# Latent attention of a decoder kernel: turns as a loop of eight, and turns written out with exponentials per head

## The chip, the cores and the metric

The kernel runs on one core of a Trainium2 chip. The metric is the device time of one execution in microseconds; three runs of the kernel before have a median of 2204.88 us (2204.24 to 2206.10). The program is one launch that holds a whole stack of four layers; the change is in one of its eight stages, with a small part moved into the set-up at the start.

## The reference

x is 4 sequences of 512 tokens with 128 features, the context 4 times 77 keys with 128 features. Each of the four layers adds a cross attention and a feed-forward of experts to x. The stage that changes is the cross attention of layer 1:

```python
xn = layernorm(context, ln_x_g, ln_x_b); ln = layernorm(x, ln_l_g, ln_l_b)
q = (ln @ Wq)                                       # 16 heads of 64
kv = concat([xn @ Wkv, ln @ Wkv], axis=1)           # 77 context keys and 512 tokens as keys
qn = rmsnorm(q, qn_g) * 64 ** -0.5; kn = rmsnorm(k, kn_g)
sim = where(mask, einsum('bhid,bhjd->bhij', qn, kn), -max)
out = softmax(sim) @ v ; x = x + out.reshape(b, 512, 1024) @ Wout + bout
```

All of it is float32; products that need it are taken from a high and a low part (float32r) of each operand.

## The kernel before

The 16 heads are taken in 8 pairs, and each pair with each of the 4 sequences is a turn: 32 turns, b = turn % 4. A turn has five chunks of keys, four of 128 tokens and one of the 77 context keys (k = 4). TensorE computes transposed scores, keys down the partitions, for both heads of the pair side by side: head 0 uses partitions 0 to 63 of the operands, head 1 the others. `scores` (L1350) does three matmul pairs for a chunk and a fourth that subtracts the row maximum (`lead`), into banks 0 and 1 or 2 and 3 by turns; `exps` on ScalarE (L1517) makes probabilities of them in one instruction of 128x1024; `add` on GpSimd (L1244) sums these over the chunks in four additions; `product` (L1373) multiplies them by the values into bank 6.

The maximum comes a turn ahead: `bound` (L1330) multiplies the high parts of queries and keys of turn + 1 into banks 4 and 5, and `read_bound` on VectorE (L1616) reduces them before the next `bound` may write there; after chunk 4 a small addition of two 128x8 tiles (an ALU maximum, L1625) writes `top_wide`. Beside this TensorE has "side products" that all pass through bank 7, each waiting until the one before it has been read: keys KL and queries Q of turn + 2, the sums of squares NKL and NQL (for the norms, by a matrix of ones), values V4, the sum SUM and the output Y of turn - 1, the transpose MT of `top_wide`, and in three turns of four one of KC, NKC, VC for the context keys and values of the next pair. VectorE copies keys and queries out of the bank, scales them by the inverse norm and splits the queries (`part_queries`, L1655: `q_hat`, `q_high`, `q_low`); GpSimd splits the keys (`part_keys`, L1232, and `part_context`); ScalarE does squares, logarithms and exponentials of the norms.

Each engine's order is written out by hand as the body of a loop of eight turns (two pairs), run four times, with semaphore targets computed in registers; the names of this stage's tiles in the profile are `sb_L_...`. The last passes also do KL, Q and bounds for turns that do not exist, whose results nobody uses. A prologue ahead of the loop norms the context and the tokens, clears tiles on GpSimd and does the first side products. `move` copies each pair's split weights inside SBUF from a store to a place of fixed address.

Of the kernel before, what the change touches and what calls it, by code (L numbers as in the profile page):

```python
# [23 lines left out]
P = 128  # L24
# [87 lines left out]
def constants(c):  # L112

    nc, d = c.nc, c.dram
    loaded, built = c.sem("loaded"), c.sem("built")
    counts = c.ctx.enter_context(nc.sbuf_tensor("counts", [P, 12], mybir.dt.int32))
    with nc.Block() as block:
        @block.sync
        def _(sp):
            sp.dma_start(c.resid[:], d["x"]).then_inc(loaded, 16)  # L120
            sp.dma_start(c.vecs[:], d["vecs"]).then_inc(loaded, 16)
            sp.dma_start(c.rows[:], d["rows"]).then_inc(loaded, 16)
            sp.dma_start(c.ctxT[:], d["ctxT"]).then_inc(loaded, 16)
            sp.wait_ge(loaded, 64)

        @block.gpsimd
        def _(pool):
# [15 lines left out]
            step(pool.memset(c.pairsum[64:128, 64:128], 1.0))  # L143


class Norm:
# [27 lines left out]
    def vector(self, dve):  # L174
# [32 lines left out]
        for b in range(BATCH if self.split else 0):  # L207
            self.wait(dve, b)
            at = slice(b * SEQ, (b + 1) * SEQ)
            step(dve.tensor_copy(self.high[:, at], c.normT[:, at]))  # L210
            dve.tensor_tensor(self.low[:, at], c.normT[:, at], self.high[:, at], ALU.subtract).then_inc(self.parted, 1)
# [10 lines left out]
    def scalar(self, act):  # L222
        act.wait_ge(self.var_ready, 1)
        act.activation(self.std[:], self.work[:, 1, :], ACT.Sqrt).then_inc(self.std_ready, 1)
        if self.inner_eps is not None:
            act.wait_ge(self.var_ready, 2)
            act.activation(self.std2[:], self.work[:, 2, :], ACT.Sqrt).then_inc(self.std_ready, 1)
        scale = self.rstd if self.inner_eps is None else self.scale
# [866 lines left out]
def latent_attention(c):  # L1095
# [7 lines left out]
    LOOP = 2 * BATCH  # L1103

    KL, Q, NKL, NQL, V4, SUM, Y, MT, KC, NKC, VC = range(11)
    BY_DVE = (KL, Q, Y, MT, KC)
    PROLOGUE = [(KC, 0), (VC, 2), (NKC, 1), (KL, 7), (Q, 6), (NKL, 3), (NQL, 0), (V4, 1), (KL, 2), (Q, 7), (NKL, 6), (NQL, 3), (MT, 7)]
    EXTRA = (KC, NKC, VC, None)
    LOOPED = [kind for j in range(LOOP) for kind in (KL, NKL, Q, SUM, NQL, V4, EXTRA[j % BATCH], Y, MT) if kind is not None]
    STARTS = [sum(9 - (i % BATCH == BATCH - 1) for i in range(j)) for j in range(LOOP + 1)]  # L1110
    AHEAD_EXPS, AHEAD_ADDS, AHEAD_PV = 6, 4, 5

    with ExitStack() as ctx:
        norm = Norm(c, ctx, "L1", inner_eps=1e-5, gain=c.vec("L1_lg"), shift=c.vec("L1_lb"), split=True)
        w_all = c.sb(ctx, "L1_w_all", [P, PAIRS + 1, 2, P])
# [974 lines left out]
```

## Time and profile before

| what | us |
|---|---|
| median of three runs | 2204.88 |
| profiled execution | 2210.48 |
| its span, first to last instruction | 2208.6 |
| TensorE / VectorE / ScalarE / GpSimd busy in it | 1911.2 / 1267.7 / 853.2 / 678.6 |
| mean granted TensorE clock | 0.941 of 2.4 GHz |
| latent attention, first instruction to last addition | 409.3 to 1186.9 |

A time in the profile is a position from the span's start. The row of an instruction has its start and duration, and in brackets how long its engine was idle ahead of it and what ended that. A matmul's end is modelled. In a stage where four engines work in a fixed order, a busy share does not say who is waited for; the rows of one turn, engine by engine, do.

### The profile page before, as it was taken

What the parts mean: (1) busy time and instruction counts of PE and PEld (TensorE: products, weight loads), DVE (VectorE), ACT (ScalarE), POOL (GpSimd) and SP (SyncE); (2) the same over time, 40 slices, a digit from 0 to 9 for tenths busy, and PEclk for the clock granted to TensorE, in tenths of its full rate; (3) what the DMA queues carried; (4) which work ended last, traced back from release to release, by engine and by line L of the source; (5) the groups of instructions that cost most, each with busy time, mean ns of one, the idle gap of its engine ahead of it and who ended that gap; (6) DMA issues with size and microseconds to landing.
All of it is one profiled execution on the core that took longest, in us unless ns stands there. A gap on an engine that the chain in (4) does not pass through costs nothing. (4 is left out here: it accounts for less than half of the span.)

```text
span 2208.6 us, 35547 instructions
## 1 busy us (share of the span) xinstructions
PE 1911.2 (87%) x12346; PEld 1335.2 (60%) x12346; DVE 1267.7 (57%) x2588; ACT 853.2 (39%) x1278; POOL 678.6 (31%) x458
## 2 busy tenths in 40 slices
PE   4978999479989989998996999959869999969798
PEld 2547999334444444444443788835546789947697
DVE  4755111556656565655665544459779975547533
ACT  2553434245545544554554222225510030045443
POOL 3321110335555564655563011033321222012110
PEclk9997999779999999999998899979979999979899
DMA  1000000100000000000000000000010000000000
GB/s 35 1 15 7 28 19 10 35 0 8 8 2 8 8 2 8 1 8 9 1 3 20 11 19 19 10 17 1 1 30 19 24 29 15 0 20 0 15 20 29
DMA packets 19844, 28.54 MB, mean 13 GB/s; under 512 B 3356, under 2 KB 13497, under 8 KB 19462
## 3 DMA queue, kind: packets, MB, share of 16 engines
q1 hardware_dynamic: 19718, 26.86, 3.9%
q8 instruction: 79, 1.29, 0.2%
q14 instruction: 47, 0.39, 0.1%
HBM read 23.71 MB, written 1.05 MB: 11 GB/s over the span
## 5 line engine op out<-in xcount | busy, mean ns | idle before, releaser
L1253 POOL TENSOR_TENSOR sb_L_total<-sb_L_total,sb_L_probT 128x1024 f32<-128x1024 f32 (+1 forms) x96 | 227.5, 2370 | 127.1 <-ACT sb_L_probT L1527 64.7
L1619 DVE TENSOR_REDUCE sb_L_top_tok<-banks 128x2 f32<-128x1024 f32 x132 | 161.8, 1226 | 81.2 <-PE banks L1339 81.1
L1525 ACT ACTIVATE sb_L_probT<-banks 128x1024 f32<-128x1024 f32 x128 | 130.0, 1015 | 120.1 <-PE banks L1370 112.3
L350 POOL TENSOR_TENSOR sb_L_prob<-sb_L_prob,sb_L_rsum 128x616 f32<-128x616 f32 (+1 forms) x96 | 98.1, 1045 | 227.0 <-DVE sb_L_rsum L566 227.0
L1380 PE MATMUL banks<-sb_L_probT,sb_L_v 128*64 128x512 f32 x520 | 138.2, 611 | 0.0
L1919 DVE SCALAR_TENSOR_TENSOR sb_L2f_hid<-banks,sb_L2f_weight,sb_L2f_hid 128x512 f32<-128x512 f32 x192 | 134.7, 744 | 3.2 <-PE banks L88 1.9
L1018 ACT ACTIVATE sb_L0f_hidden<-banks,sb_L0f_b 128x512 f32<-128x512 f32 x128 | 87.8, 689 | 112.8 <-PE banks L88 111.5
L1046 DVE SCALAR_TENSOR_TENSOR sb_resid<-banks,sb_L0f_weight,sb_resid 128x128 f32<-128x128 f32 x128 | 36.1, 344 | 164.5 <-PE banks L966 163.9
L1249 POOL TENSOR_TENSOR sb_L_total<-sb_L_probT 128x1024 f32<-128x1024 f32 x32 | 76.2, 2380 | 163.7 <-ACT sb_L_probT L1525 163.7
L966 PEld LDWEIGHTS banks<-sb_L0f_w,sb_L0f_hidden 128*128 128x128 f32 x1024 | 119.7, 192 | 2.8
L492 ACT ACTIVATE sb_L_probT<-banks 77x512 f32<-77x512 f32 x160 | 89.9, 590 | 80.7 <-PE banks L402 80.7
L1015 ACT ACTIVATE sb_L1f_gate<-banks 112x512 f32<-112x512 f32 x96 | 57.4, 598 | 162.5 <-PE banks L88 162.5
L966 PE MATMUL banks<-sb_L0f_w,sb_L0f_hidden 128*128 128x128 f32 x1024 | 119.8, 275 | 0.0
L1991 DVE SCALAR_TENSOR_TENSOR sb_resid<-banks,sb_L2f_weight,sb_resid 128x128 f32<-128x128 f32 x192 | 67.4, 351 | 69.2 <-PE banks L88 50.5
L388 PE MATMUL banks<-sb_L_kdiag,sb_L_qT 128*128 (+2 forms) x192 | 85.2, 586 | 17.2 <-DVE sb_L_prob L557 9.0
L966 PEld LDWEIGHTS banks<-sb_L1f_w,sb_L1f_hidden 112*128 112x128 f32 x768 | 92.1, 195 | 7.5 <-DVEq L1076 4.4
L966 PE MATMUL banks<-sb_L1f_w,sb_L1f_hidden 112*128 112x128 f32 x768 | 92.5, 278 | 3.9 <-DVEq L1076 3.9
L1060 DVE TENSOR_TENSOR sb_L1f_hidden<-sb_L1f_gate,banks 112x512 f32<-112x512 f32 x96 | 65.8, 687 | 49.5 <-PE banks L88 47.1
L402 PE MATMUL banks<-sb_ident,sb_L_prob 128*77 128x128 f32 x640 | 93.1, 280 | 0.0
L86 PE MATMUL banks<-sb_L2f_w_high,sb_L2f_norm_low 128*128 128x512 f32 x192 | 81.6, 425 | 9.8 <-DVE sb_L2f_hid L1919 9.6
L86 PE MATMUL banks<-sb_L2f_w_high,sb_L2f_hidT_low 128*128 128x384 f32 x256 | 86.3, 337 | 1.7 <-DVEq L1982 1.7
L88 PE MATMUL banks<-sb_L2f_w_high,sb_L2f_hidT_high 128*128 128x384 f32 x256 | 86.1, 336 | 0.0
(460 smaller groups left out, 4589.6 us busy)
## 6 DMA issues: line engine op xcount, KB each, us to landing
sb_L2f_w<-L2f_w SPq DMA_DIRECT2D x12, 256.0 KB, 2.6
sb_L2f_w<-L2f_w SPq DMA_DIRECT2D x4, 768.0 KB, 4.3
sb_L1f_w<-L1f_gu SPq DMA_DIRECT2D x8, 336.0 KB, 3.0
sb_L0f_w<-L0f_w SPq DMA_DIRECT2D x8, 259.0 KB, 2.7
sb_L0f_w<-L0f_w SPq DMA_DIRECT2D x8, 256.0 KB, 2.9
sb_L1f_w<-L1f_dn SPq DMA_DIRECT2D x8, 168.0 KB, 2.9
sb_L3f_w<-L3f_w SPq DMA_DIRECT2D x9, 129.0 KB, 2.1
sb_L3f_w<-L3f_w SPq DMA_DIRECT2D x9, 128.0 KB, 2.2
```

Of the source, the lines that this page charges most:

```text
L86: pe.matmul(out, sl, mh, start=start, stop=False)
L88: return pe.matmul(out, sh, mh, start=False, stop=stop)
L350: pool.tensor_tensor(grid, grid, bcast(rsum[:, i % PROBS, half], [None, KEYS]), ALU.mult).then_inc(normed, 1)
L402: last = pe.transpose(ps[0:KEYS, TURN + g % 2, a * P:(a + 1) * P], prob[:, i, h * KEYS:(h + 1) * KEYS], c.ident[:])
L492: act.activation(probT[:, g * GROUP:(g + 1) * GROUP, :].rearrange("k h t -> k (h t)"), ps[0:KEYS, TURN + g % 2, :], ACT.Copy).then_inc(tur ...
L966: last = pe.matmul(ps[:, YBANK + b % 2, t * P:(t + 1) * P], hid[:, b % 2, f, t * P:(t + 1) * P], w2[:, u, f, :], start=(f == 0), stop=(f = ...
L1018: act.activation(hid[:, b % 2, f, :], ps[0:R, slot, :], func, bias=bias).then_inc(hid_ready, 1)
L1253: pool.tensor_tensor(sums[rows], sums[rows], probT[rows, k], ALU.add).then_inc(added, 1)
L1380: last = pe.matmul(O[HEAD[h]], v[:, w, k, HEAD[h]], probT[:, k, h, :], start=(k == 0), stop=False)
L1525: act.activation(probT[:, k], ps[:, slot:slot + 2, :], ACT.Exp).then_inc(exped, 1)
L1619: ins = dve.tensor_reduce(top_tok[:, :, k:k + 1].rearrange("p h k -> p (h k)"), ps[:, 4:6, :], AX.X, ALU.max)
L1919: dve.scalar_tensor_tensor(out=hid[:, n, :], in0=ps[:, n % BANKS, :], scalar=flat[:, bass.ds(n * L + e, 1)], in1=hid[:, n, :], op0=ALU.mul ...
```

## The change

- The loop of eight turns becomes 32 turns written out, with constant semaphore targets; work for turns that do not exist is left out. All pairs' weights stay in SBUF, loaded once.
- `exps` makes one instruction per head, and `scores` and `product` wait and signal per head.
- TensorE's `bound` of chunk 4 stands behind V4, product 0 and the side product of the context, and VectorE's `read_bound` of chunk 4 behind `scale_context` and `part_queries`. The copy of the context keys goes from VectorE to ScalarE.
- The context's norm, transposes and clears (`LatentContext`) run in the set-up block at the kernel's start; x is loaded behind the context there.
- In the prologue the bounds of turn 0 use two pairs of banks, and GpSimd splits the first pair's weights first and the others behind the keys of turn 1; VectorE splits the last two sequences' tokens behind the queries of turn 1.

```diff
@@ -109,19 +109,21 @@
     return ap.broadcast_to(shape)
 
 
-def constants(c):
+def constants(c, early):
 
     nc, d = c.nc, c.dram
-    loaded, built = c.sem("loaded"), c.sem("built")
+    loaded, built, vecs_in, ident_ready = c.sem("loaded"), c.sem("built"), c.sem("vecs_in"), c.sem("ident_ready")
     counts = c.ctx.enter_context(nc.sbuf_tensor("counts", [P, 12], mybir.dt.int32))
+    made = LatentContext(c, early)
     with nc.Block() as block:
         @block.sync
         def _(sp):
+            sp.dma_start(c.vecs[:], d["vecs"]).then_inc(vecs_in, 16)
+            made.sync(sp)
             sp.dma_start(c.resid[:], d["x"]).then_inc(loaded, 16)
-            sp.dma_start(c.vecs[:], d["vecs"]).then_inc(loaded, 16)
             sp.dma_start(c.rows[:], d["rows"]).then_inc(loaded, 16)
             sp.dma_start(c.ctxT[:], d["ctxT"]).then_inc(loaded, 16)
-            sp.wait_ge(loaded, 64)
+            sp.wait_ge(loaded, 48)
 
...
+            pool.engine_nop().then_inc(ident_ready, 1)
+            made.gpsimd(pool)
+
+        @block.tensor
+        def _(pe):
+            pe.wait_ge(ident_ready, 1)
+            made.tensor(pe)
+
+        @block.scalar
+        def _(act):
+            made.scalar(act, vecs_in)
+
+        @block.vector
+        def _(dve):
+            dve.wait_ge(ident_ready, 1)
+            made.vector(dve, vecs_in)
+
+    return made
 
...
-            step(dve.tensor_copy(self.high[:, at], c.normT[:, at]))
-            dve.tensor_tensor(self.low[:, at], c.normT[:, at], self.high[:, at], ALU.subtract).then_inc(self.parted, 1)
+        self.step = step
+        for b in range(parts if self.split else 0):
+            self.part(dve, b)
+
...
+class LatentContext:
...
+    def tensor(self, pe):
+        pe.wait_ge(self.staged, 1)
+        for b in range(BATCH):
+            last = pe.transpose(self.c.ps[:, 0, b * KEYS:(b + 1) * KEYS], self.stage[:, b, :], self.c.ident[0:KEYS, 0:KEYS])
+        last.then_inc(self.turned, 1)
...
+        w_all, wv, wo = c.sb(ctx, "L1_w_all", [P, PAIRS, 2, P]), c.sb(ctx, "L1_wv", [P, PAIRS, P]), c.sb(ctx, "L1_wo", [P, PAIRS, P])
+        w_high, w_low = (c.sb(ctx, f"L1_w_{n}", [P, PAIRS, 2, P], F32R) for n in ("high", "low"))
...
-                def scores(turn, j, b, u, w, k, lead_read=None):
-                    n = turn * CHUNKS + k
-                    pe.wait_ge(exped, n - 1 + AHEAD_EXPS)
-                    slot = (j * CHUNKS + k) % 2 * 2
+                def scores(turn, k):
+                    n, p, b = turn * CHUNKS + k, turn // BATCH, turn % BATCH
+                    slot, rows = n % 2 * 2, rows_of(k)
                     if k < TPB:
-                        rows = P
                         high, low = (x[:, b, k * P:(k + 1) * P] for x in (k_high, k_low))
                     else:
-                        rows = KEYS
-                        high, low = (x[:, u, b, 0:KEYS] for x in (kc_high, kc_low))
-                    at = [ps[0:rows, slot + h, :] for h in range(2)]
+                        high, low = (x[:, p % 2, b, 0:KEYS] for x in (kc_high, kc_low))
+                    to = [ps[0:rows, slot + h, :] for h in range(2)]
                     for h in range(2):
-                        pe.matmul(at[h], low[HEAD[h]], q_high[HEAD[h], b, :], start=True, stop=False)
+                        if n >= 2:
+                            pe.wait_ge(exped, (n - 2) * 2 + h + 1)
+                        pe.matmul(to[h], low[HEAD[h]], q_high[HEAD[h], b, :], start=True, stop=False)
                     for h in range(2):
-                        pe.matmul(at[h], high[HEAD[h]], q_low[HEAD[h], b, :], start=False, stop=False)
+                        pe.matmul(to[h], high[HEAD[h]], q_low[HEAD[h], b, :], start=False, stop=False)
                     for h in range(2):
-                        pe.matmul(at[h], high[HEAD[h]], q_high[HEAD[h], b, :], start=False, stop=False)
+                        pe.matmul(to[h], high[HEAD[h]], q_high[HEAD[h], b, :], start=False, stop=False)
                     if k == 0:
-                        pe.wait_ge(dve_read, lead_read)
+                        wait_read(pe, MT, turn)
                     for h in range(2):
-                        last = pe.matmul(at[h], ones[HEAD[h], 0:rows], lead[HEAD[h], w, :], start=False, stop=True)
-                    last.then_inc(scored, 1)
-
-                def product(turn, b, u, w, k):
-                    n = turn * CHUNKS + k
-                    pe.wait_ge(exped, n + 1 + AHEAD_EXPS)
-                    if k == 0:
-                        pe.wait_ge(mixed_ready, turn + 1)
+                        pe.matmul(to[h], made.ones[HEAD[h], 0:rows], lead[HEAD[h], turn % 2, :], start=False, stop=True).then_inc(scored, 1)
+
+                def product(turn, k):
+                    p, b = turn // BATCH, turn % BATCH
+                    if k == 0 and turn > 0:
+                        pe.wait_ge(mixed_ready, turn)
                     for h in range(2):
+                        pe.wait_ge(exped, (turn * CHUNKS + k) * 2 + h + 1)
                         if k < TPB:
-                            last = pe.matmul(O[HEAD[h]], v[:, w, k, HEAD[h]], probT[:, k, h, :], start=(k == 0), stop=False)
+                            last = pe.matmul(O[HEAD[h]], v[:, turn % 2, k, HEAD[h]], probT[:, k, h, :], start=(k == 0), stop=False)
                         else:
-                            last = pe.matmul(O[HEAD[h]], vc[:, u, b, HEAD[h]], probT[0:KEYS, k, h, :], start=False, stop=True)
+                            last = pe.matmul(O[HEAD[h]], vc[:, p % 2, b, HEAD[h]], probT[0:KEYS, k, h, :], start=False, stop=True)
                     last.then_inc(pv_done, 1)
...
+                    scores(turn, 3)
+                    if more:
+                        bound(turn + 1, 3)
+                        use_side(V4, turn + 1)
+                    product(turn, 0)
+                    if p + 1 < PAIRS and b < BATCH - 1:
+                        use_side((KC, NKC, VC)[b], p + 1)
+                    if more:
+                        bound(turn + 1, 4)
+                    scores(turn, 4)
+                    if turn > 0:
+                        use_side(Y, turn - 1)
+                    product(turn, 1)
+                    if more:
+                        use_side(MT, turn + 1)
...
+                def exps(turn, k):
                     n = turn * CHUNKS + k
-                    slot = (j * CHUNKS + k) % 2 * 2
-                    rows = slice(0, P if k < TPB else KEYS)
-                    act.wait_ge(scored, n + 1)
-                    act.wait_ge(pv_done, n - CHUNKS + 1 + AHEAD_PV)
...
+                    for h in range(2):
+                        act.wait_ge(scored, n * 2 + h + 1)
+                        if k < TPB:
+                            ins = act.activation(probT[:, k, h], ps[:, slot + h, :], ACT.Exp)
+                        else:
+                            ins = act.activation(probT[rows, k, h], ps[rows, slot + h, :], ACT.Exp, bias=made.barredT[:, turn % BATCH:turn % BATCH + 1])
+                        ins.then_inc(exped, 1)
...
+                part_weights(0, 1)
+                part_context(0)
+                part_keys(0)
+                pool.wait_ge(w_in, 16)
+                part_keys(1)
+                part_weights(1, PAIRS)
...
-                        read_bound(turn + 1, 0, base)
-                        take_keys(at(KL), w)
-                        read_bound(turn + 1, 1, base)
-                        take_queries(at(Q), turn + 2)
-                        read_bound(turn + 1, 2, base)
+                for turn in range(TURNS):
+                    more, much = turn + 1 < TURNS, turn + 2 < TURNS
+                    if more:
+                        read_bound(turn + 1, 0)
+                    if much:
+                        take_keys(turn + 2)
+                    if more:
+                        read_bound(turn + 1, 1)
+                    if much:
+                        take_queries(turn + 2)
+                    if more:
+                        read_bound(turn + 1, 2)
+                    if turn > 0:
                         mix(turn - 1)
-                        scale_keys(turn + 2, w)
-                        read_bound(turn + 1, 3, base)
-                        read_bound(turn + 1, 4, base)
-                        if b == 0:
-                            dve.wait_ge(kc_ready, g * 2 + u + 1)
-                            take_context(at(KC))
-                        if b == 2:
-                            scale_context(g * 2 + u + 1)
-                        part_queries(turn + 2, (b + 2) % BATCH, reads_before(g, j, Q, True) + 1, base)
-                        add_result(at(Y), (b - 1) % BATCH)
-                        take_lead(at(MT), turn + 1, 1 - w)
-                end = use_of(TURNS // LOOP, 0, KL)
+                    if much:
+                        scale_keys(turn + 2)
+                    if more:
+                        read_bound(turn + 1, 3)
+                    if turn % BATCH == 2 and turn // BATCH + 1 < PAIRS:
+                        scale_context(turn // BATCH + 1)
+                    if much:
+                        part_queries(turn + 2)
+                    if more:
+                        read_bound(turn + 1, 4)
+                    if turn > 0:
+                        add_result(turn - 1)
+                    if more:
+                        take_lead(turn + 1)
```

VectorE in a turn of the loop, from the reduction of chunk 3 (`top_tok`) to the addition of the output (`sb_resid`), before:

```order
L1619 TENSOR_REDUCE sb_L_top_tok<-banks 128x2
L1617 REGISTER_ALU
L1622 TENSOR_REDUCE sb_L_top_ctx<-banks 128x8
L1625 TENSOR_TENSOR sb_L_top_wide<-sb_L_top_tok,sb_L_top_ctx 128x2x4
L1657 REGISTER_ALU
L1659 SCALAR_TENSOR_TENSOR sb_L_q_hat<-sb_L_q_inv,sb_L_q_raw 128x512
L100 REGISTER_ALU
L1660 CAST sb_L_q_high<-sb_L_q_hat 128x512
L100 REGISTER_ALU
L1661 TENSOR_TENSOR sb_L_q_low<-sb_L_q_hat,sb_L_q_high 128x512
L1669 REGISTER_ALU
L1671 TENSOR_TENSOR sb_resid<-banks,sb_resid 128x512
```

and now:

```order
L1634 TENSOR_REDUCE sb_L_top_tok<-banks 128x2
L1669 SCALAR_TENSOR_TENSOR sb_L_q_hat<-sb_L_q_inv,sb_L_q_raw 128x512
L1670 CAST sb_L_q_high<-sb_L_q_hat 128x512
L1671 TENSOR_TENSOR sb_L_q_low<-sb_L_q_hat,sb_L_q_high 128x512
L1636 TENSOR_REDUCE sb_L_top_ctx<-banks 128x8
L1638 TENSOR_TENSOR sb_L_top_wide<-sb_L_top_tok,sb_L_top_ctx 128x2x4
L1682 TENSOR_TENSOR sb_resid<-banks,sb_resid 128x512
```

The reduction of the context chunk and `top_wide` have moved from ahead of the three query steps to behind them.

TensorE in a turn with b = 0, from the bound of chunk 3 (out of `sb_L_k_high`), before. The rows with `sb_L_barred` and `sb_L_kc_high` are the bound of chunk 4, `sb_L_wv,sb_normT` is V4, `sb_L_probT` product 0:

```order
L1339 MATMUL banks<-sb_L_k_high,sb_L_q_high 128x512 x2
L1336 REGISTER_ALU
L1342 MATMUL banks<-sb_L_barred,sb_L_ones 128x312 x2
L1346 MATMUL banks<-sb_L_kc_high,sb_L_q_high 128x78 x8
L1425 REGISTER_ALU
L1303 ISA
L1307 MATMUL banks<-sb_L_wv,sb_normT 64x128 x8
L1380 MATMUL banks<-sb_L_probT,sb_L_v 64x512 x2
```

and now, where `sb_L_cT` is the context keys' side product KC:

```order
L1390 MATMUL banks<-sb_L_k_high,sb_L_q_high 128x512 x2
L1358 MATMUL banks<-sb_L_wv,sb_normT 64x128 x8
L1430 MATMUL banks<-sb_L_probT,sb_L_v 64x512 x2
L86 MATMUL banks<-sb_L_cT_high,sb_L_w_low 128x308
L87 MATMUL banks<-sb_L_cT_low,sb_L_w_high 128x308
L88 MATMUL banks<-sb_L_cT_high,sb_L_w_high 128x308
L1394 MATMUL banks<-sb_L_barred,sb_L_ones 128x312 x2
L1398 MATMUL banks<-sb_L_kc_high,sb_L_q_high 128x78 x8
```

The bound of chunk 4 has moved behind V4, product 0 and KC, and the register instructions are gone.

## Rows read from the trace of the kernel before

**Rows 1.** The table of waits, 478 to 1182 us: who waited for whom, us, times, longest.

```profile
PE banks L1342 <- DVE sb_L_top_tok L1619: 42.4, 32, 1.3
```

**Rows 2.** Timeline of TensorE in one turn: start us, us, engine, line, operation [idle before].

```profile
595.95 0.50 PE L1362 MATMUL banks<-sb_L_q_high,sb_L_k_low 64*128 64x512 f32 x2
596.28 0.40 PE L1364 MATMUL banks<-sb_L_q_low,sb_L_k_high 64*128 64x512 f32 x2
596.52 0.39 PE L1366 MATMUL banks<-sb_L_q_high,sb_L_k_high 64*128 64x512 f32 x2
...
598.70 0.42 PE L1342 MATMUL banks<-sb_L_barred,sb_L_ones 64*128 64x312 f32 x2 [1.32 <-DVE sb_L_top_tok L1619]
...
599.42 1.09 PE L1307 MATMUL banks<-sb_L_wv,sb_normT 128*64 128x128 f32 x16
...
601.29 0.74 PE L1286 MATMUL banks<-sb_L_kc_sq,sb_pairsum 128*64 128x308 f32 x4
601.96 0.46 PE L1362 MATMUL banks<-sb_L_q_high,sb_L_kc_low 64*77 64x512 f32 x2
...
605.19 0.50 PE L1362 MATMUL banks<-sb_L_q_high,sb_L_k_low 64*128 64x512 f32 x2
```

**Rows 3.** Timeline of VectorE in the same turn.

```profile
597.42 1.23 DVE L1619 TENSOR_REDUCE sb_L_top_tok<-banks 128x2 f32<-128x1024 f32 x1 [0.45 <-PE banks L1339]
599.53 0.81 DVE L1622 TENSOR_REDUCE sb_L_top_ctx<-banks 128x8 f32<-128x624 f32 x1 [0.89 <-PE banks L1346]
600.38 1.40 DVE L1625 TENSOR_TENSOR sb_L_top_wide<-sb_L_top_tok,sb_L_top_ctx 128x8 f32<-128x8 f32 x1
601.70 0.68 DVE L1659 SCALAR_TENSOR_TENSOR sb_L_q_hat<-sb_L_q_inv,sb_L_q_raw 128x512 f32<-128x512 f32 x1
...
602.87 0.69 DVE L1661 TENSOR_TENSOR sb_L_q_low<-sb_L_q_hat,sb_L_q_high 128x512 fp32r<-128x512 f32 x1
```

**Rows 4.** Timeline of GpSimd in the same turn.

```profile
598.17 1.27 POOL L1235 TENSOR_TENSOR sb_L_k_low<-sb_L_k_raw,sb_L_k_high 128x512 fp32r<-128x512 f32 x1
599.39 2.36 POOL L1253 TENSOR_TENSOR sb_L_total<-sb_L_total,sb_L_probT 128x1024 f32<-128x1024 f32 x1
604.51 2.38 POOL L1253 TENSOR_TENSOR sb_L_total<-sb_L_total,sb_L_probT 77x1024 f32<-77x1024 f32 x1 [2.76 <-ACT sb_L_probT L1527]
```

**Rows 5.** Timeline of VectorE and GpSimd in the latent attention's prologue.

```profile
454.38 1.04 POOL L1234 TENSOR_TENSOR sb_L_k_high<-sb_L_k_raw,sb_one 128x512 fp32r<-128x512 f32 x1
454.39 1.58 DVE L1659 SCALAR_TENSOR_TENSOR sb_L_q_hat<-sb_L_q_inv,sb_L_q_raw 128x512 f32<-128x512 f32 x1 [0.61 <-ACT sb_L_q_inv L1501]
...
455.50 1.59 POOL L1235 TENSOR_TENSOR sb_L_k_low<-sb_L_k_raw,sb_L_k_high 128x512 fp32r<-128x512 f32 x1
456.01 1.37 DVE L1660 CAST sb_L_q_high<-sb_L_q_hat 128x512 fp32r<-128x512 f32 x1
```

**Rows 6.** Timeline of TensorE: first scores of turns 0, 8 and 30.

```profile
475.71 0.79 PE L1362 MATMUL banks<-sb_L_q_high,sb_L_k_low 64*128 64x512 f32 x2
...
653.00 0.79 PE L1362 MATMUL banks<-sb_L_q_high,sb_L_k_low 64*128 64x512 f32 x2 [4.83 <-issue]
...
1136.51 0.50 PE L1362 MATMUL banks<-sb_L_q_high,sb_L_k_low 64*128 64x512 f32 x2
```

**Rows 7.** Timeline of VectorE: first statistics of two layers, last addition of the latent attention.

```profile
7.81 3.18 DVE L177 BATCH_NORM_STATS2 sb_L_stats<-sb_resid 128x6 f32<-128x128 f32 x16
...
429.72 3.18 DVE L177 BATCH_NORM_STATS2 sb_L_stats<-sb_resid 128x6 f32<-128x128 f32 x16
...
1186.19 0.69 DVE L1671 TENSOR_TENSOR sb_resid<-banks,sb_resid 128x512 f32<-128x512 f32 x1 [1.32 <-PE banks L1315]
```

**Rows 8.** Timeline of SyncE: first instruction of the latent attention.

```profile
409.28 0.33 SPq L1172 DMA_DIRECT2D sb_L_cx<-ctx  x1
```

**Rows 9.** Stretch: us, busy PE, PEld, DVE, ACT, POOL, clock, DMA; bias addition on POOL.

```profile
418.60:426.90 8.30, 0.00 (x0) 0.00 (x0) 7.99 (x5) 0.20 (x1) 8.12 (x3) 0.50 0.00 0
...
466.08 4.51 POOL L1258 TENSOR_TENSOR sb_resid<-sb_resid,sb_rows 128x2048 f32<-128x2048 f32 x1
```

More of the change, by code:

```diff
@@ L1258, in _ @@
[L1258 to L1271 removed]
+                pool.wait_ge(first_in, 16)
@@ L1328, in use_side, with bound @@
                     last.then_inc(side_done, 1)
-                def bound(turn, b, u, k, first=False):
+                def bound(turn, k, banks=4):
+                    p, b = turn // BATCH, turn % BATCH
                     if k == 0:
@@ L1334, in bound @@
                         pe.wait_ge(q_ready, turn + 1)
-                    if not (first and k == 0):
-                        pe.wait_ge(bound_read, turn * CHUNKS + k)
+                    if banks == 4 and turn + k > 0:
+                        pe.wait_ge(bound_read, turn * CHUNKS + k - (turn == 0))
                     if k < TPB:
                         for h in range(2):
-                            last = pe.matmul(ps[:, 4 + h, :], q_high[HEAD[h], b, k * P:(k + 1) * P], k_high[HEAD[h], b, :], start=True, stop=True)
+                            last = pe.matmul(ps[:, banks + h, :], q_high[HEAD[h], b, k * P:(k + 1) * P], k_high[HEAD[h], b, :], start=True, stop=True)
@@ L1579, in _ @@
+                    exps(turn, 4)
+                invert_sum(TURNS - 1)
             @block.vector
             def _(dve):
-                cstep = InOrder(dve, corder)
-                dve.wait_ge(ctx_in, 16)
-                for b in range(BATCH):
-                    last = dve.bn_stats(cstats[:, b, :], cx[:, b, :])
-                cstep(last)
-                half, gap, spread, var, std, mean = (cwork[:, i, :] for i in range(6))
-                dve.tensor_tensor(half, cstats[:, :, 1], cstats[:, :, 4], ALU.add)
@@ L1714, in _ @@
-                end = use_of(TURNS // LOOP, 0, KL)
+                scale_keys(0)
+                take_keys(1)
+                part_queries(0)
+                take_queries(1)
+                scale_keys(1)
+                read_bound(0, 0)
+                read_bound(0, 1, 0)
+                read_bound(0, 2)
+                read_bound(0, 3, 0)
+                read_bound(0, 4)
+                take_lead(0)
+                part_queries(1)
+                norm.part(dve, 2)
+                norm.part(dve, 3)
@@ L2020, in program @@
             c.retire(taken)
+            if step is steps[2]:
+                early.close()
         stored = c.sem("stored")
```

715 lines of the change are left out of this document (331 added, 384 removed).

## Prediction

> **What bounds the kernel now.** I read the page first, then the idle table and the timelines of one turn in the middle of the latent attention, which runs from 409.28 to 1186.88 us [rows 6, 7]. There the reader is to see that TensorE's rows follow each other without a gap but for one: the bound of the context keys starts 1.32 us late, because the four banks' pair it writes is still being reduced by VectorE [rows 2]; the idle table has it 32 times, 42.4 us in all [rows 1]. So TensorE sets the pace. The second thing is the start of each later pass of the loop: TensorE waits 4.83 us for nothing that the profile shows, and its first matmul pair then takes 0.79 us where it took 0.50 [rows 2, 6]. Last I looked at VectorE against GpSimd. A VectorE operation that has its inputs in SBUF does not run while a GpSimd add runs: `top_wide`, 8 elements wide, takes 1.40 us and ends when the add that started at 599.39 and took 2.36 has ended [rows 3, 4]. In the prologue `q_hat` (0.68 us when alone) took 1.58 and `q_high` 1.37 (alone it fits into the 0.49 between the end of `q_hat` at 602.38 and `q_low` at 602.87), and they took turns with `k_high` and `k_low`, one VectorE operation per GpSimd operation [rows 3, 5]. Reductions and additions that read a bank (`top_tok`, 1.23 us, and the `resid` addition) are not held. In the old order only `top_wide` meets an add; `q_hat` starts at 601.70, when the add is over, and `q_low` ends at 603.56, before the next add at 604.51 [rows 3, 4]. The new order gives this up.
>
> **The loop written out.** The old time from the first scores at 475.71 to those of turn 30 at 1136.51 is 660.8 us [rows 6], with three changes of pass in it. Each costs the 4.83 us of waiting and about 1.6 us at the lower clock level (the scores, the bound and one product run at 1.2 GHz until the clock is granted again, by the 0.79 against 0.50 of the pair): 6.4 us, three times 19 us. It goes, as nothing branches any more. Whether a long straight stream is fetched in time the trace does not show: between nothing and one such wait per eight turns, which would give the 19 us back. I take nothing, since it is behind the branch that the 4.83 us stand, and not within the eight turns of a pass. The copies of each pair's weights inside SBUF, and the loads of its value and output weights, go with the loop; TensorE waited for none of them. The copy of the context keys moves from VectorE to ScalarE, 0.5 us in one turn of four, beside other work on both.
>
> **The gap of 1.32 us.** The bound of the context keys moves behind V4, a product and the side product. These take 599.42 to 601.96, 2.54 us [rows 2], more than the 1.23 us of the reduction [rows 3], so this wait is covered. It is what VectorE and TensorE then wait for that matters.
>
> **The exponentials head by head.** Ten instructions per turn of half the size instead of five, and a wait ahead of each head's first matmul. TensorE waits for no exponential in a steady turn, so an earlier first half buys nothing. The price: a matmul pair behind a wait has 0.33 us to the next pair and the pair after it 0.24 [rows 2], so 0.1 us a wait; ten more waits per turn, seven of them before the scores of chunk 3. Bounds: nothing (register instructions go at the same places) and 0.24 us each (the heads lose their overlap). I take 0.1 us, and as TensorE already waits a little for k_sq, q_raw and the logarithm of the sum, 0.4 us of the 0.7 reach chunk 3. Per instruction ScalarE pays some 0.1 us more per pair, off the path. Each head's last matmul now raises the semaphore too. The Trainium skill (TensorE: Matmul & The Clock Gate, "The cost: per-tile semaphore tail") puts each extra increment at 26 ns; no row of this trace shows two of them, and by it the sum would be 4 us higher (160 increments).
>
> **VectorE's new order, worked through for the turn of rows 2 to 4.** All times are the old ones plus the shift of 0.4. The reduction of chunk 3 starts at 597.8 and ends at 599.05. Now `part_queries` follows instead of the context reduction. `k_low` ends at 599.85 (the add starts behind it at 599.39 in the old trace): `q_hat` waits for that and ends at 600.4 (0.55 us past the release, as 455.42 to 455.97 in rows 5). The add of chunk 3 then holds the port until 602.6; `q_high` ends 0.3 later at 602.9, `q_low` 603.55. The context reduction (0.81) ends at 604.35. TensorE meanwhile: V4 from 597.8, product and side product 2.54 + 0.1, bound 0.72, scores of chunk 4 from 601.25. In the old trace the last add starts 2.55 us behind these scores (604.51 against 601.96); with a wait and two exponentials 2.75, at 604.0. So `top_wide`, due at 604.35, meets the add (2.38) and ends at 606.4. `add_result` 0.69, 607.1; the transpose needs both, and the next turn's scores start at 607.4 instead of 605.19: +2.2 us. TensorE, ready at about 604.7, stands for 2.4 us instead of 1.3.
> The Trainium skill (SBUF — State Buffer, "Who interferes with whom") says the same of this port: an operation with two SBUF inputs, a cast, and a GpSimd operation that reads SBUF exclude each other for a whole instruction, in issue order, and a reduction is never held.
>
> **The other turns of a pair of heads.** Turn b=0 is like this one: +2.2. For b=3 no side product stands ahead of the last scores, the add comes earlier and `top_wide` surely behind it, +2.3. For b=2 the scaling of the context keys goes first; `q_hat` falls behind the add of chunk 3 and the next two behind the two context splits: between +2.2 (as the others) and +3.6 (three more waits); I take +2.5, since that stage's idle time on GpSimd shrinks. Together 9.2 us per pair, seven pairs 64 us; turns 28 and 29, which lose their side products, +1.7 each. 64 + 3 - 19 = +48 us up to turn 30.
>
> **The last two turns** take 1136.51 to 1186.88, 50.4 us [rows 6, 7]. The new ones do no work for turns that do not exist. Turn 30 loses four side products of 0.93 us (599.42 to 601.29 holds two such pieces) and the gap: about 17. Turn 31 is set by GpSimd: 4.8 us to its first add, four adds of 2.38, then sum, logarithm, exponential, mix, output and addition, an estimate of 5: 19.4. 36.4 in all, -14 us.
>
> **The prologue** took 409.28 to 475.71, 66.4 us. The context's norm goes to the kernel's start, so the token statistics start 20.4 us earlier (429.72 [rows 7]). Not all is kept. TensorE waits for the last of four loads (2 MB) at about 8 us and does the context values before the transposes: N = 10 us, where it could be 8. From there the chain through ScalarE's ten activations and VectorE brings the bounds of turn 0 to N+17 and `top_wide` to N+23, and there GpSimd has the other seven weights (7/8 of the 8.1 us in the window of rows 9) and the bias addition of 4.51 us one behind the other. VectorE's last two query steps and four norm steps get one slot each between these, so the first scores wait until N+35 = 45 us: -21 us. Bounds: -28 (everything as in the old spacing from the statistics on, less the port) and -12.
>
> **The kernel's start.** Vectors, context and masks are issued ahead of x, some 2 us, and the context chain (DMA, statistics, root, transposes, split) took 20.4 us with about 10 of it standing behind GpSimd's clears and splits [rows 8, 9]; without these it ends at 11.5, against 7.81 now [rows 7]: +4 us, between +2 (x alone) and +9 (all clears in the way).
>
> **Sum:** +48 - 14 - 21 + 4 = +17 us on the profiled execution's 2210.5. That execution is 5.6 us above the median of the runs (its span 2208.6 and 1.9 around it); a change of stages moves both alike, so 2204.9 + 17 = 2222 us.
>
> **Rivals.**
> 1. *The race of `top_wide` is won in b=0 and b=1.* My margin is 0.35 us (604.0 against 604.35); 0.35 us more on TensorE between chunks 3 and 4, or less on VectorE, lets `top_wide` through. Then add_result ends at 605.1 and the turn is +0.3 instead of +2.2: 14 turns, -27 us, 2195 us, faster than before. For it: the small margin, and waits dearer than 0.1 us push the add, not the reduction. Against it: cheaper waits do the contrary.
> 2. *The port hardly matters* (GpSimd's operations slip between VectorE's, or VectorE gets in early): TensorE sets the turn, which loses the 1.32 us and gains at most 1.0 in waits, and 0.7 in b=3: 30 turns -26 us, less 19, -45; with -14 - 21 + 4 that is -76, 2129 us. Against it stand the rows of 1.40, 1.58 and 1.37 us; it decides if `q_high` is found under 0.5 us.
> 3. *The longer standstill costs the clock too.* In b=2 TensorE would stand 3.5 to 4 us per turn, near the 4.83 us behind which the clock was at the lower level, while 1.32 us did not lower it. 1.6 us in seven turns: +11, 2233 us.
>
> **How the numbers follow.** Forecast 0.47, rival 1 0.25, rival 2 0.20, rival 3 0.08. What can be told from no change here is 0.2%, 4.4 us. The forecast's own range, with the bounds of prologue and start, is 2206 to 2240. With rivals 1 and 3 it is 2180 to 2245, which leaves out rival 2. Faster: rival 2 and most of rival 1, 0.40. Same: the edges of forecast and rival 1, 0.08. Slower 0.52.
>
> **What would show it.** In the new trace: `q_high` at 2 us or more and `top_wide` at 2 us in most turns; TensorE's transpose of `top_wide` waiting about 2.5 us each turn for `sb_resid`, and no wait at the context bound; turns of 23 to 24.5 us; no 4.8 us waits; first scores about 45 us into the stage; the last two turns in 36 to 37 us. The forecast is wrong if `q_high` stays under 0.5 us, or if the wait at the transpose is under 1 us in two of four turns.

## The result, and the profile after

The changed kernel takes 2267.86 us (median of 4 runs, 2265.55 to 2269.14), the kernel before 2205.49 us (4 runs, 2204.24 to 2206.4): the ratio is 1.0282, interval 1.0264 to 1.0300. It is slower, as forecast, but by 62 us and not by 17, outside the range of 2180 to 2245. All times here are those of fast executions; one of experiment 4, which took 4799.44 us where the other three took 2227 to 2237, is left out.

The page of the changed kernel: span, the busy time of each engine, and the clock in 40 slices (lines between them left out).

```profile
span 2265.7 us, 33399 instructions
PE 1933.8 (85%) x12232; PEld 1351.4 (60%) x12232; DVE 1331.7 (59%) x2557; ACT 856.4 (38%) x1426; POOL 679.4 (30%) x447
PEclk8997999789988999998998799979979999979799
```

VectorE's busy time rose by 64 us although it does fewer instructions: an operation that is held counts as busy. TensorE's rose by 22.6 us with 114 matmuls fewer: the slices that hold the turns show a clock of 8 or 9 where they all showed 9. The table of waits, 440 to 1240 us, answers [rows 1]:

```profile
PE banks L1369 <- DVE sb_resid L1682: 96.2, 29, 4.0
PE banks L1413 <- DVE sb_L_norm_low L235: 11.4, 1, 11.4
```

The standstill at the context bound is gone; in its place TensorE stands ahead of the transpose of `top_wide` in every turn, 96.2 us in all against 42.4. One turn (b=1) as TensorE sees it, against [rows 2]:

```profile
677.45 0.40 PE L1369 MATMUL banks<-sb_ident,sb_L_top_wide 128*128 128x128 f32 x1 [2.66 <-DVE sb_resid L1682]
677.78 0.79 PE L1413 MATMUL banks<-sb_L_q_high,sb_L_k_low 64*128 64x512 f32 x2
678.38 0.63 PE L1415 MATMUL banks<-sb_L_q_low,sb_L_k_high 64*128 64x512 f32 x2
...
695.13 0.41 PE L1394 MATMUL banks<-sb_L_barred,sb_L_ones 64*128 64x312 f32 x2
...
701.46 0.48 PE L1369 MATMUL banks<-sb_ident,sb_L_top_wide 128*128 128x128 f32 x1 [2.71 <-DVE sb_resid L1682]
```

The first pair of scores takes 0.79 us, the next 0.63; in [rows 2] they took 0.50 and 0.40. A view by stretch (us, busy times, granted clock) of the beginning of the next turn says why:

```profile
701.50:704.00 2.50, 2.50 (x11) 1.62 (x11) 0.69 (x1) 0.00 (x0) 0.00 (x0) 0.50 0.00 0
704.00:706.00 2.00, 2.00 (x8) 0.68 (x7) 1.23 (x1) 1.08 (x2) 0.00 (x0) 0.78 0.00 0
706.00:720.00 14.00, 13.63 (x92) 6.79 (x90) 8.38 (x9) 9.04 (x16) 8.29 (x5) 1.00 0.01 2
```

At 0.50 TensorE has the lower level, 1.2 GHz. It falls behind the standstill, in every turn. VectorE in the same turn, against [rows 3]:

```profile
692.79 1.23 DVE L1634 TENSOR_REDUCE sb_L_top_tok<-banks 128x2 f32<-128x1024 f32 x1 [0.49 <-PE banks L1390]
693.93 1.39 DVE L1669 SCALAR_TENSOR_TENSOR sb_L_q_hat<-sb_L_q_inv,sb_L_q_raw 128x512 f32<-128x512 f32 x1
695.35 2.50 DVE L1670 CAST sb_L_q_high<-sb_L_q_hat 128x512 fp32r<-128x512 f32 x1
697.88 0.69 DVE L1671 TENSOR_TENSOR sb_L_q_low<-sb_L_q_hat,sb_L_q_high 128x512 fp32r<-128x512 f32 x1
698.49 0.80 DVE L1636 TENSOR_REDUCE sb_L_top_ctx<-banks 128x8 f32<-128x624 f32 x1
699.33 1.47 DVE L1638 TENSOR_TENSOR sb_L_top_wide<-sb_L_top_tok,sb_L_top_ctx 128x8 f32<-128x8 f32 x1
700.72 0.68 DVE L1682 TENSOR_TENSOR sb_resid<-banks,sb_resid 128x512 f32<-128x512 f32 x1
```

And GpSimd, against [rows 4]:

```profile
693.50 1.28 POOL L1289 TENSOR_TENSOR sb_L_k_low<-sb_L_k_raw,sb_L_k_high 128x512 fp32r<-128x512 f32 x1
694.73 2.83 POOL L1307 TENSOR_TENSOR sb_L_total<-sb_L_total,sb_L_probT 128x1024 f32<-128x1024 f32 x1
698.32 2.46 POOL L1307 TENSOR_TENSOR sb_L_total<-sb_L_total,sb_L_probT 77x1024 f32<-77x1024 f32 x1 [0.76 <-ACT sb_L_probT L1584]
```

`q_high` ends with the addition of chunk 3 and `top_wide` with that of chunk 4. In a turn b=3 it is `q_low` that meets the last addition, and `top_wide` runs free:

```profile
649.09 2.75 DVE L1671 TENSOR_TENSOR sb_L_q_low<-sb_L_q_hat,sb_L_q_high 128x512 fp32r<-128x512 f32 x1
651.77 0.79 DVE L1636 TENSOR_REDUCE sb_L_top_ctx<-banks 128x8 f32<-128x624 f32 x1
652.60 0.17 DVE L1638 TENSOR_TENSOR sb_L_top_wide<-sb_L_top_tok,sb_L_top_ctx 128x8 f32<-128x8 f32 x1
```

TensorE's first scores of turns 0 and 30, SyncE's first instruction of the stage and VectorE's last addition answer [rows 6 to 8]:

```profile
457.30 0.79 PE L1413 MATMUL banks<-sb_L_q_high,sb_L_k_low 64*128 64x512 f32 x2 [11.36 <-DVE sb_L_norm_low L235]
...
1200.37 0.79 PE L1413 MATMUL banks<-sb_L_q_high,sb_L_k_low 64*128 64x512 f32 x2
```

```profile
409.74 0.34 SPq L1270 DMA_DIRECT2D sb_L_w_all<-L_w  x1
```

```profile
1236.20 0.69 DVE L1682 TENSOR_TENSOR sb_resid<-banks,sb_resid 128x512 f32<-128x512 f32 x1 [1.28 <-PE banks L1366]
```

With these the two executions are compared term by term:

| Term | forecast | measured | from |
|---|---|---|---|
| kernel's start | +4 | +0.5 | 409.74 against 409.28 |
| prologue | -21 | -18.9 | 47.56 against 66.43 |
| turns 0 to 29 | +48 | +82.3 | 743.07 against 660.80 |
| last two turns | -14 | -13.9 | 36.52 against 50.37 |
| behind the latent attention | 0 | +7.1 | 57.1 (spans) less the 50.0 above |

One term is far off, and it is the largest. The first and the last rest on one execution each, and kernels with the same code there differ by as much (see "The start" and "Behind the latent attention").

### The profile page after: what moved, and what is told of

Read it like the earlier page. It is cut to its first block and busy times, and to the rows that moved or that the text cites. A ratio compares the mean times of both kernels' runs of the same rounds, so it can differ in the third digit from the quotient of the medians.

```text
span 2265.7 us, 33399 instructions
## 1 busy us (share of the span) xinstructions
PE 1933.8 (85%) x12232; PEld 1351.4 (60%) x12232; DVE 1331.7 (59%) x2557; ACT 856.4 (38%) x1426; POOL 679.4 (30%) x447
## 5 line engine op out<-in xcount | busy, mean ns | idle before, releaser
L1307 POOL TENSOR_TENSOR sb_L_total<-sb_L_total,sb_L_probT 128x1024 f32<-128x1024 f32 (+1 forms) x96 | 243.1, 2532 | 75.5 <-ACT sb_L_probT L1582 61.4
L1582 ACT ACTIVATE sb_L_probT<-banks 128x512 f32<-128x512 f32 x256 | 137.8, 590 | 238.2 <-PE banks L1421 238.2
L1634 DVE TENSOR_REDUCE sb_L_top_tok<-banks 128x2 f32<-128x1024 f32 x128 | 156.4, 1224 | 92.1 <-PE banks L1390 92.1
L1430 PE MATMUL banks<-sb_L_probT,sb_L_v 128*64 128x512 f32 x512 | 149.2, 662 | 0.1
L1369 PE MATMUL banks<-sb_ident,sb_L_top_wide 128*128 128x128 f32 x32 | 13.5, 422 | 101.8 <-DVE sb_resid L1682 96.2
L992 PEld LDWEIGHTS banks<-sb_L1f_w,sb_L1f_hidden 112*128 112x128 f32 x768 | 92.9, 196 | 9.0 <-DVEq L1102 6.0
```

Source lines behind the costliest of these rows:

```text
L992: last = pe.matmul(ps[:, YBANK + b % 2, t * P:(t + 1) * P], hid[:, b % 2, f, t * P:(t + 1) * P], w2[:, u, f, :], start=(f == 0), stop=(f = ...
L1307: pool.tensor_tensor(sums[rows], sums[rows], probT[rows, k], ALU.add).then_inc(added, 1)
L1430: last = pe.matmul(O[HEAD[h]], v[:, turn % 2, k, HEAD[h]], probT[:, k, h, :], start=(k == 0), stop=False)
L1582: ins = act.activation(probT[:, k, h], ps[:, slot + h, :], ACT.Exp)
L1634: dve.tensor_reduce(top_tok[:, :, k:k + 1].rearrange("p h k -> p (h k)"), ps[:, banks:banks + 2, :], AX.X, ALU.max).then_inc(bound_read, 1)
```

## The experiments

All ran beside the kernel before on the same chip, which had medians of 2206.35, 2208.49 and 2206.74 us in the three groups.

**1. The old place of the context bound in the changed kernel.**

```
  TensorE:  bound(turn + 1, 3)
+           bound(turn + 1, 4)
            use_side(V4, turn + 1); product(turn, 0); side product
-           bound(turn + 1, 4)
  VectorE:  read_bound(turn + 1, 3)
+           read_bound(turn + 1, 4)
            scale_context; part_queries(turn + 2)
-           read_bound(turn + 1, 4)
```

> The changed kernel, in which only the place of the context bound is as it was: on TensorE the context bound follows the bound of chunk 3 again, on VectorE its reduction and top_wide stand ahead of the three query steps again. Everything else (no loop, exponentials by head, new prologue) stays. Theory, the order on VectorE meets GpSimd's last add and costs the clock: turns fall back to the 21.3 us of the kernel before, without the three changes of pass, so turns 0 to 29 take about 640 us where the changed kernel takes 742.9; 2268 - 103 = 2165 us, with TensorE standing 1.3 us a turn at the context bound and the clock high. Rival, the length of the stream or the exponentials by head make the turns long: they stay above 23 us, and the time above 2230.

2161.93 us, ratio to the kernel before 0.9792 (0.9766 to 0.9817). A pair of heads (four turns) takes 85.6 us where the changed kernel's takes 99.0, and the clock of the turns is 1.00. So 106 us of the changed kernel's time are this order alone, and all the rest of the change is a gain of 44 us.

**2. Exponentials in one instruction again.**

```
- for h in range(2): wait scored n*2+h+1; activation(probT[:, k, h], ps[:, slot+h])
+ wait scored n+1; activation(probT[:, k], ps[:, slot:slot+2])
  scores, product: one wait and one signal for both heads again
```

> The changed kernel with the exponentials of both heads in one instruction and one semaphore step again, and nothing else. Theory (the order is what costs): TensorE waits for no exponential, so nothing moves much: 2258 to 2272 us, since the turn is set by the chain of VectorE and GpSimd, which starts 0.1 to 0.2 us earlier at best. Rival, each wait ahead of a head's matmul costs TensorE 0.1 us as I had put it: ten a turn are 30 us over 30 turns, 2238 us.

2265.82 us, 1.027 (1.0245 to 1.0295), not to be told from the changed kernel's 2267.86. So my 0.1 us per wait did not count here; as VectorE and GpSimd set the turn in this kernel, a small cost on TensorE would not show.

**3. V4 between the two bounds**, on top of experiment 1.

```
  bound(turn + 1, 3)
+ use_side(V4, turn + 1)
  bound(turn + 1, 4)
- use_side(V4, turn + 1)
  product(turn, 0)
```

> As the kernel with the old order, but TensorE computes the values (V4) between the bound of chunk 3 and the context bound; the product and the side product stay behind the latter. The 0.9 us of V4 lie in the 1.32 us that TensorE stood there. Theory: the turn is set by TensorE, and loses 0.9 to 1.0 us of standing: 28 us less than with the old order, about 2137 us. Rival, the chain of VectorE and GpSimd sets the turn there too: within 5 us of the kernel with the old order.

2151.17 us, 0.9748 (0.972 to 0.9775): 11 us less than the first experiment, where 28 were expected. The wait at the context bound fell from 42.4 to 10.7 us, but 14.7 us came back at the transpose, behind VectorE's addition to `sb_resid`. No turn is shorter than 20.7 us, most take 20.76, and TensorE stands in each of them, so something else sets them; experiment 5, without two of GpSimd's additions, comes down to 19.3. Neither theory had this size.

**4. Filling the standstill.** Ten matmuls whose results are overwritten stand ahead of the transpose:

```
  product(turn, 1)
+ wait for the exponentials of chunk 3, the last that read this bank
+ for _ in range(10):
+     pe.matmul(ps[:, next scores' bank], ones, q_high[:, b, :])
  use_side(MT, turn + 1)
```

> The changed kernel with ten matmuls of 128x512 that nobody reads, put into each turn ahead of the transpose of top_wide, into the banks that the next scores start anew. They only fill the time in which TensorE stood there (2.7 to 4.0 us a turn). Theory, about 34 us of the loss are TensorE's lower clock behind each standstill: the clock of turns 0 to 29 stays near 1 where it was 0.91, and the time falls by 20 to 34 us, to 2234 to 2248, though ten matmuls were added to every turn. Rival, the loss is all waiting for VectorE and GpSimd: 2268 us or more.

2233.06 us, 1.0115 (1.0075 to 1.0156): 35 us less than the changed kernel, for more work. The fill, what is left of the standstill, and the scores behind it at full speed:

```profile
689.68 2.60 PE L1518 MATMUL banks<-sb_L_q_high,sb_L_ones 128*128 128x512 f32 x10
692.51 0.33 PE L1369 MATMUL banks<-sb_ident,sb_L_top_wide 128*128 128x128 f32 x1 [0.24 <-DVE sb_resid L1685]
692.78 0.50 PE L1413 MATMUL banks<-sb_L_q_high,sb_L_k_low 64*128 64x512 f32 x2
```

The clock of turns 0 to 29, then the same stretch of the changed kernel (columns as above):

```profile
459.50:1162.30 702.80, 664.12 (x4245) 340.95 (x4245) 486.31 (x455) 348.26 (x603) 383.77 (x194) 0.99 0.00 1
```

```profile
457.30:1200.20 742.90, 630.55 (x3943) 311.00 (x3943) 484.05 (x454) 348.04 (x603) 381.81 (x194) 0.91 0.00 1
```

The turns b = 0 to 3 take 22.7, 22.7, 24.1 and 23.5 us instead of 24.0, 24.0, 25.3 and 25.7. From the transpose ahead of turn 1 to that ahead of turn 30 it is 679.5 us against 720.3. So the clock costs at least 41 us; three turns b=0 still took 24.3, behind a lower clock.

**5. Without the additions of chunks 3 and 4** (the row sums lack these chunks).

```
+ elif k > 2:
+     pool.wait_ge(added, ...); pool.engine_nop().then_inc(added, 1)
```

> The changed kernel without the last two of GpSimd's four additions of a turn (the sums lack chunks 3 and 4); VectorE's and TensorE's orders stay as changed. Theory (VectorE's operations wait for these additions): q_high falls from 2.49 us to about 0.45, q_low to 0.7, top_wide to 0.2, TensorE sets the turn at 20.0 to 20.8 us, its clock stays up, and the time is about 2268 - 30 x 4.1 = 2145 us, at least below 2160. Rival, the length of VectorE's own chain behind chunk 3 sets the turn, additions or not: turns above 22.5 us, 2225 or more.

2114.81 us, 0.9574 (0.9556 to 0.9593). The cast's instructions in the steady turns (shortest, median, longest in ns), here and in the changed kernel:

```profile
L1673 DVE CAST sb_L_q_high<-sb_L_q_hat x29: 426/427/809, 490.6 to 1047.8; 128x512 fp32r<-128x512 f32 x29
```

```profile
L1670 DVE CAST sb_L_q_high<-sb_L_q_hat x29: 804/2491/2507, 497.5 to 1193.1; 128x512 fp32r<-128x512 f32 x29
```

TensorE stands nowhere in a steady turn, and turns take 19.3 to 20.5 us. 153 us less, 30 more than expected: I had put the turn at 20.0 to 20.8.

**6. `top_wide` by a reduction.**

```
- tensor_tensor(top_wide, top_tok, top_ctx, max)
+ tensor_reduce(top_wide, tops[P, 2, TPB, 2], max)   # both maxima side by side
```

> The changed kernel, in which top_wide is made by a reduction over pairs (token maximum, context maximum) instead of by an operation with two inputs in SBUF. Theory (a reduction is not held by an addition, as those that read a bank are not): top_wide falls from 1.47 to about 0.2 us in the turns b = 0, 1 and 2, the transpose comes 1.3 us earlier there, nothing changes in b = 3 where q_low meets the addition: 22 turns by 1.3 are 29 us, and some of the clock on top, 2225 to 2240 us. Rival, a reduction whose input lies in SBUF is held like the others: top_wide stays at 1.4 us, 2268 us.

2212.81 us, 1.0017 (1.0 to 1.0034): 55 us less than the changed kernel for one instruction's form. Its durations, and those of the old form in the changed kernel:

```profile
L1638 DVE TENSOR_REDUCE sb_L_top_wide<-sb_L_tops x28: 169/170/171, 501.9 to 1123.2; 128x8 f32<-128x16 f32 x28
```

```profile
L1638 DVE TENSOR_TENSOR sb_L_top_wide<-sb_L_top_tok,sb_L_top_ctx x29: 166/1470/1474, 501.5 to 1199.1; 128x8 f32<-128x8 f32 x29
```

The transposes come 1.3 us earlier in 22 turns, 29 us; the rest of the gain is clock, which was 0.95 over the turns where it had been 0.91. The standstills are now 1.37, 1.37, 2.28 and 4.02 us at the ends of the turns b = 0 to 3, and a turn b=1, with short ones on both sides, takes 21.3 us.

**7. The new order in the kernel before**, with its loop, its exponentials and its prologue. The edit is that of the change: `bound_next(4)` behind the side product, `read_bound(turn + 1, 4)` behind `part_queries`.

> The kernel before (loop, exponentials in one instruction, old prologue) with only the new place of the context bound: on TensorE behind V4, the product and the side product, on VectorE its reduction and top_wide behind the three query steps. Theory: the order alone costs what the two kernels' turns differ by (98.97 against 85.27 us a pair of heads), eight times 13.7 are 110 us, so about 2205 + 105 = 2310 us, with q_high at 2.5 and top_wide at 1.5 us and the clock low behind each standstill. Rival, it needs the exponentials by head or the straight stream as well: under 2260 us.

2316.55 us, 1.0495 (1.0467 to 1.0523): the order alone costs 108 us, and needs neither the straight stream nor the exponentials by head.

**8. A shorter prologue**, on top of experiment 3.

```
  GpSimd:   part_keys(1)
+           norm.wait_parts(pool)       # all four norm splits
            part_weights(1, PAIRS)      # then the bias addition
  TensorE: -norm.wait_parts(pe); wait w_parted 2   (ahead of turn 0)
           +norm.wait_parts(pe, turn + 2)          (ahead of keys 2 and 3)
           +wait w_parted 2                        (first side product)
  VectorE: scale_context behind read_bound(turn + 1, 1)
           wait bias_added ahead of the first add_result
```

> The kernel with V4 between the bounds, and three changes more: GpSimd splits the seven later heads' weights and adds the bias behind the four norm splits of VectorE instead of ahead of them (TensorE waits for them at the first side product, VectorE ahead of its first addition); TensorE waits for the third and fourth norm split only ahead of the keys that use them; the context keys are scaled between the first and second chunk's reductions instead of between the third's and the query steps. Theory: the 11.4 us that TensorE stood ahead of its first scores fall to 2 or less, as q_hat, q_high and q_low of turn 1 take 1.8 us in all instead of 8.5 (-9 us); in turns b = 2 the 0.93 us of standing go, and 1.2 us of TensorE's turn (22.0 to 20.8), seven times 1.2 (-8 us): 2151 - 17 = 2134 us. Rival, the splits and the bias addition, moved beside the first turn, hold VectorE's key operations there and cost as much: 2140 us or more.

2143.69 us, 0.9695 (0.9668 to 0.9722), 7 us less than experiment 3 where 17 were expected. This is the fastest kernel that computes everything, faster than both. VectorE's cast of turn 1 (and GpSimd beside it) in the changed kernel, and here:

```profile
449.18 4.94 POOL L1316 TENSOR_TENSOR sb_resid<-sb_resid,sb_rows 128x2048 f32<-128x2048 f32 x1
449.80 4.60 DVE L1670 CAST sb_L_q_high<-sb_L_q_hat 128x512 fp32r<-128x512 f32 x1
```

```profile
446.99 0.43 DVE L1672 CAST sb_L_q_high<-sb_L_q_hat 128x512 fp32r<-128x512 f32 x1
```

The first scores come at 445.56 instead of 457.30 (457.90 in experiment 3), but turn 0 then takes 3.7 us longer than in experiment 3, from its first scores to those of turn 1. In the turns b=2 only 0.4 us of the 1.2 were won (21.6 instead of 22.0), since the moved operation meets another addition (2.60 us). The last addition of the stage comes 11.3 us earlier than in experiment 3, some 1.5 us of that because the stage began earlier; what follows it took 3.8 us more. Both are taken up below.

**9 and 10. The product ahead of the context bound too**, with the exponentials by head and in one instruction.

```
  use_side(V4, turn + 1)
- bound(turn + 1, 4)
  product(turn, 0)
+ bound(turn + 1, 4)
```

> The kernel with the short prologue, in which TensorE does the product of chunk 0 ahead of the context bound as well as V4; VectorE's order stays. TensorE still stood 0.35 us a turn at that bound (12.0 us in all) for the reduction of chunk 3. Theory: top_wide ends with GpSimd's addition of chunk 3 in any case, so a context bound that starts 0.65 us later costs VectorE nothing, and TensorE keeps the 0.35 us: 30 turns, 10 us, 2133 us. Rival, the turn is set by the addition that ends ahead of q_hat and by the query steps behind it: the 0.35 us come back as standing at the transpose, 2141 to 2145 us.

> As the kernel with the product ahead of the context bound, but the exponentials of both heads in one instruction and one semaphore step, as in the kernel before. Theory (what the exponentials by head cost or bring is under 4 us either way, as in the changed kernel, where one instruction gave 2265.8 against 2267.9): within 5 us of its time. Rival, now that TensorE sets most of the turn, the additions start 0.07 to 0.15 us earlier with one instruction and free VectorE earlier: 5 us or more faster.

2180.08 us, 0.9886 (0.9862 to 0.9909), and 2174.5 us, 0.9848 (0.9825 to 0.9872): both 31 to 36 us slower than experiment 8. I had missed this in both theories. In the turns b = 1 and 2 nothing moved (20.8 and 21.6 us: the 0.35 us came back at the transpose, as the rival said). In b=3, with no side product, TensorE now reaches the last scores early enough for GpSimd to start the last addition ahead of `q_low`:

```profile
616.51 2.62 POOL L1307 TENSOR_TENSOR sb_L_total<-sb_L_total,sb_L_probT 77x1024 f32<-77x1024 f32 x1 [0.66 <-ACT sb_L_probT L1587]
```

```profile
616.98 2.71 DVE L1674 TENSOR_TENSOR sb_L_q_low<-sb_L_q_hat,sb_L_q_high 128x512 fp32r<-128x512 f32 x1
```

The addition starts 0.47 us ahead of `q_low`; in experiment 8 it started 0.16 us behind it (616.87 against 616.71). Counted from the transpose ahead of the turn, `q_low` stands where it stood, and the addition comes 0.6 us earlier. Now TensorE stands 3.40 us, the clock falls, and that turn and the next take 22.8 and 23.4 us, where experiment 8 had 20.8 each. One instruction for the exponentials gave 5.6 us less, on overlapping intervals; this is left open.

## Why the prediction was right in sign and wrong in size

**VectorE's new order: right.** Queries ahead of the context reduction meet GpSimd's additions, one VectorE operation per addition. The Trainium skill (SBUF — State Buffer, "Who interferes with whom") says that a VectorE operation with two SBUF inputs, or a cast that uses both ports, and a GpSimd operation that reads SBUF exclude each other, the first of them for its whole instruction, and that on this chip a reduction never contends. The runs agree: the cast 2.49 against 0.43 us without the additions (experiment 5), and `top_wide` 1.47 against 0.17 us by a reduction whose input lies in SBUF too (6). Rival 2 (the port hardly matters) fell with these rows. I had the wrong partner in b=3: `q_low`, not `top_wide`. That the price came near the forecast (+2.8 us with the standstill filled, against +2.3) is luck.

**The turns' length without the clock: nearly right.** The old turns took 21.4, 21.3, 21.9 and 20.7 us; with the shifts forecast for them that makes 23.6, 23.5, 24.4 and 23.0. With the standstills filled they are 22.7, 22.7, 24.1 and 23.5, together 92.9 where I had 94.5. The waits per head, 0.4 us a turn in my sum, are the likely difference. Undoing them changed nothing (2), and in experiment 1, whose turns have them in the old order, four turns take 85.6 us against 85.3 in the kernel before: 0.1 us a turn, not 0.4.

**What failed: the clock, which the forecast priced at nothing and rival 3 at 11 us and in b=2 alone.** I read that 4.83 us of standing lowers the clock and 1.32 does not, and put the bound between them close to the upper end. The runs put it lower. Standstills of up to 1.41 us left the clock up (6). Behind the nine of 1.54 to 1.56 us it fell in three turns, some 1.5 us into the turn, and behind one of 1.87 us it stayed up (4). Behind the seven of 2.27 to 2.29 us it fell in four (6): in two of them by the first scores, in the two others only some 2 us behind the transpose, where the duration of the first scores does not show it. From those two turns (columns as above):

```profile
803.00:805.00 2.00, 2.00 (x5) 0.39 (x4) 1.05 (x1) 0.62 (x2) 0.00 (x0) 0.50 0.00 0
895.00:897.00 2.00, 2.00 (x6) 0.83 (x3) 0.65 (x1) 0.36 (x1) 0.00 (x0) 0.50 0.00 0
```

Behind all 29 of the changed kernel, 2.65 to 4.03 us, it fell, and by the turns of experiment 4 each turn paid 1.2 to 2.2 us for it, 41 us in all. That is the whole miss of the turns: 82.3 less 41 is 41, against 48 forecast. Of the 45 us between 17 and 62, the turns are 34; 7 lie behind the latent attention, 5 are what the profiled execution before lay above its median, and start, prologue and last turns together take 1 off. The forecast had itself put 2.4 us of standing into every turn; rival 3's condition should have been asked of that number, not only of the longest.

**Rival 1** did not come: `top_wide`, due 0.35 us behind the last addition, was 1.01 us behind it (699.33 against 698.32).

**The loop, prologue and last turns: right.** My terms for all but the order were -19, -21, -14 and +4, together -50 us (the range that I gave beside them, 2206 to 2240, begins 3 us lower than its bounds and the 4.4 us make it: 2209). Experiment 7 against the changed kernel gives 2316.55 less 2267.86, -49; experiment 1 against the kernel before gives -44. The straight stream brought no waits for instructions. In the prologue TensorE waited for the last load at 9.9 us (N = 10) and 11.4 us for the norm splits, as described.

**The start** was delayed by 2.3 us (first statistics at 10.06 instead of 7.81) and gave it back within the first layer: the first group of its six score matmuls took 2.34 us where it took 4.48. Why is open, as the profile gives both stretches a granted clock of 1.00. The +0.5 us of the table is no measure of the change either: the stage began at 407.0 us (experiment 10) to 412.7 us (4) in kernels with the same code ahead of it.

**Behind the latent attention** the 7.1 us cannot be laid to any part of the change. From the last addition of the stage to the end of the span the kernels with identical code there took 1020.6 (experiment 5) to 1030.9 us (4), without relation to what was edited; the kernel before took 1021.7, the changed one 1028.8. This also blurs gains below 10 us, as that of experiment 8.

## What to carry to other kernels

Before an operation of VectorE is moved, lay it against GpSimd's operations at the new time. Here a cast or an operation with two SBUF inputs lasted until the addition that it met had ended (2.49 against 0.43 us, 1.47 against 0.17), a reduction did not (0.17), and 0.6 us decided which operation met it. When a forecast contains a standstill of TensorE in every turn, price it twice, as waiting and as the slow matmuls behind it (here 1.2 to 2.2 us for standstills of 2.65 us and more). A wait removed from TensorE pays only until the next engine's chain, here 20.76 us a turn, takes over.

## What the runs showed that I had not expected

- Ten useless matmuls a turn made the kernel 35 us faster (2267.86 to 2233.06).
- The form of one instruction over 8 elements, a reduction in place of an operation with two inputs, was worth 55 us (2267.86 to 2212.81).
- Letting TensorE reach the last scores of a turn 0.6 us earlier cost 36 us (2143.69 to 2180.08).
